# Layer 2 of the first two output tiles in seven block products, in a two-layer MLP with a residual

## The reference

```python
IN, HID, OUT, PART, E = (512, 2048, 512, 128, 8)
x = ...                         # (16, 512, 512) float32
itok_B_0_7 = ...                # 16 indices in 0..7
...
h = jax.nn.gelu(jnp.einsum('bni,ih->bnh', x, W1) + b1, approximate=False)
shared_x = jnp.einsum('bnh,ho->bno', h, W2) + b2      # W2: 2048 x 384
expert_x = jnp.einsum('bnh,bhp->bnp', h, We[indices]) + be[indices][:, None, :]   # 2048 x 128
return x + jnp.concatenate([shared_x, expert_x], axis=-1)
```

## Time and profile before

| | us |
|---|---|
| median of 3 runs (1288.54 to 1289.84) | 1289.72 |
| the profiled execution | 1288.96 |
| its span, first to last instruction | 1287.2 |
| PE busy | 1271.1 |
| DVE busy | 691.7 |
| ACT busy | 505.5 |
| moved by DMA | 62.23 MB, mean 48 GB/s |

### The profile page before, as it was taken

The page is one execution under the profiler, slowest core; times in us unless marked ns, Lnnn a source line. Parts: engine busy times, 40 slices in busy tenths (PEclk is TensorE's granted clock), DMA queues, the critical chain, the costliest instruction groups (busy, mean ns, idle before and its releaser), DMA issues.

```text
span 1287.2 us, 21032 instructions
## 1 busy us (share of the span) xinstructions
PE 1271.1 (99%) x8387; PEld 818.7 (64%) x8387; DVE 691.7 (54%) x860; ACT 505.5 (39%) x812; POOL 0.2 (0%) x4
## 2 busy tenths in 40 slices
PE   7999999999999999999999999999999999999998
PEld 3446666666666666666666666666666666666664
DVE  6965753745546455554645537455464555546442
ACT  3744444343343433343434443433434333434331
POOL 0000000000000000000000000000000000000000
PEclk8999999999999999999999999999999999999999
DMA  7121202011020110202001020110201102120000
GB/s 294 66 66 58 74 34 67 33 40 48 18 57 33 53 45 8 57 33 65 33 24 41 33 65 33 39 47 20 57 33 53 45 8 57 33 65 33 17 17 33
DMA packets 25081, 62.23 MB, mean 48 GB/s; under 512 B 5088, under 2 KB 5088, under 8 KB 21984
## 3 DMA queue, kind: packets, MB, share of 16 engines
q1 hardware_dynamic: 25056, 61.90, 15.1%
HBM read 45.11 MB, written 16.78 MB: 48 GB/s over the span
## 4 chain that ended last, share of the span: by engine, by line
PE 97%; DVE 2%; ACT 0%; issue 0%; ACTq 0%
PE out_ps L855 17%; PE out_ps L856 17%; PE out_ps L857 17%; PE banks L855 15%; PE banks L857 15%; PE banks L856 15%; DVE w_lo L543 1%; PE out_ps L990 1%; DVE w_max L529 0%; DVE x_lo L543 0%; DVE h_ring L543 0%; DVE x_max L529 0%; DVE e_lo L543 0%; ACT u L412 0%; ACT w_hi L369 0%
## 5 line engine op out<-in xcount | busy, mean ns | idle before, releaser
L855 PE MATMUL banks<-x_hi,w_hi 128*128 128x256 f16 (+1 forms) x1744 | 483.4, 277 | 7.6 <-DVE w_lo L543 5.0
L856 PE MATMUL banks<-x_lo,w_hi 128*128 128x256 f16 (+1 forms) x1744 | 483.2, 277 | 0.0
L857 PE MATMUL banks<-x_hi,w_lo 128*128 128x256 f16 (+1 forms) x1744 | 483.2, 277 | 0.0
L855 PE MATMUL out_ps<-h_ring,w_hi 128*128 128x512 f16 x768 | 291.0, 379 | 1.5 <-DVE w_lo L543 1.5
L857 PE MATMUL out_ps<-h_ring,w_lo 128*128 128x512 f16 x768 | 291.0, 379 | 0.0
L856 PE MATMUL out_ps<-h_ring,w_hi 128*128 128x512 f16 x768 | 291.0, 379 | 0.0
L404 ACT ACTIVATE kept<-banks 128x512 f32<-128x512 f32 x180 | 106.2, 590 | 366.2 <-PE banks L857 366.2
L855 PEld LDWEIGHTS banks<-x_hi,w_hi 128*128 128x128 f16 x1744 | 170.8, 98 | 80.1 <-DVE w_lo L543 5.2
L856 PEld LDWEIGHTS banks<-x_lo,w_hi 128*128 128x128 f16 x1744 | 170.9, 98 | 71.1 <-issue 1.1
L857 PEld LDWEIGHTS banks<-x_hi,w_lo 128*128 128x128 f16 x1744 | 170.9, 98 | 27.4 <-issue 1.4
L720 DVE TENSOR_TENSOR u<-banks,kept 128x512 f32<-128x512 f32 x60 | 41.5, 692 | 234.0 <-ACT kept L404 234.0
(11 more groups left out here) (90 smaller groups left out, 781.3 us busy)
## 6 DMA issues: line engine op xcount, KB each, us to landing
x_raw<-x_dram SPq DMA_DIRECT2D x64, 256.0 KB, 3.5
e_raw<-we_dram SPq DMA_DIRECT2D x16, 1024.0 KB, 4.7
out_dram<-x_raw SPq DMA_DIRECT2D x64, 256.0 KB, 2.0
stage<-w_dram SPq DMA_DIRECT2D x4, 1024.0 KB, 4.9
h_ring<-w_dram SPq DMA_DIRECT2D x2, 1024.0 KB, 8.6
stage<-w_dram SPq DMA_DIRECT2D x2, 768.0 KB, 14.4
x_raw<-w_dram SPq DMA_DIRECT2D x1, 1024.0 KB, 11.0
t_sum<-w_dram SPq DMA_DIRECT2D x1, 1024.0 KB, 12.5
```

What stands on the lines that cost most here:

```text
L855: nc.tensor.matmul(ps, hi, v_hi, start=start, stop=False, skip_group_check=True)
L856: nc.tensor.matmul(ps, hi, v_lo, start=False, stop=False, skip_group_check=True)
L857: return nc.tensor.matmul(ps, lo, v_hi, start=False, stop=stop, skip_group_check=True)
```

## The change

From batch 2 on (`PLAIN = 2`), layer 2 of output tiles 0 and 1 is computed by the same seven-product scheme: the 256 output columns by 512 tokens are a 2 by 2 of blocks, and the sum over the hidden features of a group likewise. It needs sums and differences of the blocks of h and of W2:

- `h_split`'s hi moves from VectorE to ScalarE for all batches. VectorE then makes four differences of blocks in place in `u` (`add_ht`, four adds of 128 x 512), ScalarE their hi, VectorE their lo (`ht_split`, 128 x 2048 each). `h_ring` now holds two groups of two parts.
- The sums of W2 are made once, in batch 2, from W2 loaded a second time (`reload_w2`, `add_w2_s`, `w2_s_split`).
- PSUM: `banks` shrinks to A and B (P5 and P3 take B, so P5 now waits for `c11` and P2 for `c12` of the step before), `out_ps` to two banks (o = 2 and 3); the seven products add up in four banks `q_ps`. `mix` (VectorE) puts them together: five passes of 128 x 256 for bank 2, two each for banks 0, 1 and 3; `q_keep` (ScalarE) copies the eighth block.
- A group's layer 2 is now 15 units: P1, P2, P6, P5, P7, P4 (six matmuls of 256 columns each), eight plain units of three matmuls with 512 columns for o = 2 and 3, then P3. `Q_UNITS` spreads them 2, 2, 3, 2, 2, 2, 2.
- The orders on VectorE and ScalarE change; `residual` moves from step 1 to step 0. The warm-up matmuls at the start become 60 and 30 with 256 columns instead of 32 and 14 with 512. The h scale has a smaller exponent.

```diff
+PLAIN = 2
-WARM, WARM_MORE = 32, 14
+WARM, WARM_MORE = 60, 30
...
-BANK_A, BANK_B, BANK_C = range(3)
-BANK = {P1: BANK_A, P2: BANK_B, P6: BANK_A, P5: BANK_C, P7: BANK_A, P4: BANK_A, P3: BANK_C}
+BANK_A, BANK_B = range(2)
+BANK = {P1: BANK_A, P2: BANK_B, P6: BANK_A, P5: BANK_B, P7: BANK_A, P4: BANK_A, P3: BANK_B}
...
+Q_PLACE = {P1: (0, 0), P2: (0, 1), P6: (1, 0), P5: (1, 1), P7: (2, 0), P4: (2, 1), P3: (3, 0)}
+Q_OPENS = (P1, P6, P7, P3)
 UNITS = (2, 2, 3, 2, 2, 3, 2)
+Q_UNITS = (2, 2, 3, 2, 2, 2, 2)
...
@@ scalar: h_split, ht_split, batch
+                nc.scalar.activation(h_ring[:, d % 2, 0, 0], u[:, d % 2].rearrange("p c n -> p (c n)"), ACT.Copy,
+                                     scale=scale[:, par, 1:2]).then_inc(h_hi_done, 1)
...
+                act.wait_ge(ht_added, 4 * (D * (b - PLAIN) + d) + 4)
+                nc.scalar.activation(h_ring[:, d % 2, 1, 0], u[:, d % 2].rearrange("p c n -> p (c n)"), ACT.Copy,
+                                     scale=scale[:, par, 1:2]).then_inc(ht_hi_done, 1)
...
                 keep(b, 0, 0)
+                h_split(b - 1, 1 - par, 3)
                 keep(b, 0, 1)
+                ht_split(b - 1, 1 - par, 3)
+                residual(b, par)
                 keep(b, 0, 2)
...
@@ vector: add_ht, mix (bank 2), batch (steps 1 to 3)
+                nc.vector.tensor_tensor(b11, b12, b11, ALU.subtract).then_inc(ht_added, 1)
+                dve.wait_ge(ht_added, base + 1)
+                nc.vector.tensor_tensor(b12, b22, b12, ALU.subtract).then_inc(ht_added, 1)
+                dve.wait_ge(ht_added, base + 2)
+                nc.vector.tensor_tensor(b22, b22, b11, ALU.subtract).then_inc(ht_added, 1)
+                dve.wait_ge(ht_added, base + 3)
+                nc.vector.tensor_tensor(b21, b21, b22, ALU.subtract).then_inc(ht_added, 1)
...
+                elif bank == 2:
+                    dve.wait_ge(q_taken, 4 * k + 2)
+                    take(c22, P7, c22).then_inc(q_mixed, 1)
+                    take(u_mix[:, :], P7, u_mix[:, :]).then_inc(q_mixed, 1)
+                    take(c21, P4, c21).then_inc(q_taken, 1)
+                    dve.wait_ge(q_mixed, 5 * k + 4)
+                    nc.vector.tensor_tensor(c22, c22, w_mix[:, :], ALU.add).then_inc(q_mixed, 1)
+                    dve.wait_ge(q_taken, 4 * k + 3)
+                    nc.vector.tensor_tensor(c21, c21, u_mix[:, :], ALU.add).then_inc(out_ready[1], 1)
...
+                c11(b, 1)
+                h_split(b, 0, par)
                 e_scales(b, par)
-                finish(b - 1, 1 - par, 0)
+                add_ht(b, 0)
+                mix(b - 1, 1 - par, 0)
                 e_split(b, 0)
+                e_split(b, 1)
+                ht_split(b, 0, par)
...
                 c22(b, 1)
...
+                c11(b, 2)
+                h_split(b, 1, par)
+                mix(b - 1, 1 - par, 2)
+                add_ht(b, 1)
+                finish(b - 1, 1 - par, 2)
                 finish(b - 1, 1 - par, 3)
-                c11(b, 2)
+                mix(b - 1, 1 - par, 3)
+                ht_split(b, 1, par)
...
                 c22(b, 2)
...
                 if loads is not None:
                     x_top(b + 1, 1 - par, loads)
-                h_split(b, par, 2)
                 c11(b, 3)
+                h_split(b, 2, par)
                 if loads is not None:
                     x_scales(b + 1, 1 - par)
+                add_ht(b, 2)
+                if loads is not None:
+                    add_t(b + 1, 1 - par)
                     x_split(b + 1, 1 - par, P1)
                     x_split(b + 1, 1 - par, P2)
-                    add_t(b + 1, 1 - par)
-                e_split(b, 3)
+                ht_split(b, 2, par)
                 c22(b, 3)
...
@@ tensor: layer1, plain_unit, product_unit
                 if i == P2 and begun:
-                    pe.wait_ge(c11_added, s)
-                if i == P5 and begun:
                     pe.wait_ge(c12_added, s)
+                if i == P5:
+                    pe.wait_ge(c11_added, s + 1)
...
+                first, last = d == 0 and c == 0, d == D - 1 and c == C - 1
...
+                if first and not (isinstance(b, int) and b == 0):
+                    pe.wait_ge(out_ready[o], b)
...
+                bank, n = Q_PLACE[i]
+                if d == 0 and n == 0:
+                    if not (isinstance(b, int) and b == PLAIN):
+                        pe.wait_ge(q_taken, 4 * (b - 1 - PLAIN) + bank + 1)
```

More of the change, by code:

```diff
@@ L180, in build, with place @@
         residual_done = sem("residual_done")
[L181 to L185, removed]
+        plain_summed = sem("plain_summed")
+        o_summed = sem("o_summed")
+        q_summed = sem("q_summed")
+        q_kept = sem("q_kept")
+        q_taken = sem("q_taken")
+        q_mixed = sem("q_mixed")
+        out_ready = [sem(f"out_ready{o}") for o in range(OT)]
+        def place(r, part):
+            return h_ring[:, r, part].rearrange("p a n -> p (a n)").bitcast(F32)
         def w1_raw(d):
@@ L289, in _ @@
             load_w1(3)
-            for d in range(D):
-                load_w2(d)
+            load_w2(0)
+            load_w2(1)
+            load_w2(3)
+            sp.wait_ge(w1_lo_done, 2)
+            load_w2(2)
             load_expert(0, 0)
@@ L740, in batch @@
+            def batch(b, par, loads=None, sums=False, w2_s=False):
                 c11(b, 0)
+                h_split(b - 1, 3, 1 - par)
+                add_ht(b - 1, 3)
                 e_top(b)
+                ht_split(b - 1, 3, 1 - par)
                 if sums:
                     add_s(1)
+                if w2_s:
+                    add_w2_s(0)
                 c22(b, 0)
-                c12(b, 0)
                 if sums:
                     s_split(1)
-                h_split(b, par, 0)
+                if w2_s:
+                    w2_s_split(0)
+                c12(b, 0)
@@ L841, in _ @@
             batch(1, 1, 1, sums=True)
+            batch(2, 0, 2, w2_s=True)
             with dve.Fori(0, B // 2 - 2) as pair:
-                batch(2 * pair + 2, 0, pair + 2)
                 batch(2 * pair + 3, 1, pair + 2)
-            batch(B - 2, 0, B // 2)
+                batch(2 * pair + 4, 0, pair + 3)
             batch(B - 1, 1)
-            h_split(B - 1, 1, 3)
-            for o in range(OT):
-                finish(B - 1, 1, o)
+            h_split(B - 1, 3, 1)
+            add_ht(B - 1, 3)
+            ht_split(B - 1, 3, 1)
+            for bank in range(3):
+                mix(B - 1, 1, bank)
+            finish(B - 1, 1, 2)
+            finish(B - 1, 1, 3)
+            mix(B - 1, 1, 3)
         @block.tensor
@@ L924, in layer2 @@
                 v = slice(c * N, (c + 1) * N)
[L925 to L934 removed]
+                ps = q_ps[:, o].rearrange("p j n -> p (j n)") if o < 2 else out_ps[:, o - 2]
@@ L998, in _ @@
             pe.wait_ge(w2_lo_done, D)
-            for d in range(D):
-                step(1, d)
-            with pe.Fori(2, B - 1) as b:
+            for b in (1, 2):
+                for d in range(D):
+                    step(b, d)
+            with pe.Fori(3, B - 1) as b:
                 for d in range(D):
@@ L1006, in _ @@
             for d in (D - 2, D - 1):
-                for unit in range(OT * C):
+                for unit in range(sum(Q_UNITS)):
                     layer2(B - 1, d, unit)
```

387 lines of the change are left out of this document (273 added, 114 removed).

## The result

| | before | after |
|---|---|---|
| median, us | 1289.2 | 1394.74 |
| ratio, with its 95% interval | | 1.082 (1.0807 to 1.0832) |
| profiled execution, us | 1288.96 | 1393.71 |
| its span, us | 1287.2 | 1391.9 |
| mean granted clock | 0.997 | 0.979 |

Each median is that of four runs; those of the change lie between 1393.71 and 1396.12 us.

The account below looks back on a forecast made before the run. PE's own rate was taken as the bound. From 1289.7 us, savings of 33.0 and 0.4 against waits of 84.0 and 11.0 in the loop, 6.85 in batch 2 and 5.3 at the end gave +73.7: 1363 us, range 1325 to 1395.

Parts of the forecast that it names:

- the course given 0.74: The main forecast: PE waits in the loop as walked through each step, 1363 us, own range 1345 to 1387, chance 0.74.
- the clock rival: Step 2's two gaps bring PE's clock to its low level each batch, costing 2.6 x 14 = 36 us: 1400, chance 0.11.
- three signs of being wrong: PE waiting under 2.4 us a batch, a 256-column pass far from 0.48, or granted clock leaving 1.0 in the loop.
- The saving on PE: Layer 2, batches 2 to 15: seven products replace eight units, 0.6 us a step over 56 groups, 33 us.
- The walk: PE's waits traced through each step: 4.46 us in step 2, 1.6 in step 0, 0.4 in step 1, 0.85 in step 3.
- step 2, P7 of layer 2 for `mix`: In step 2, PE waits for the `mix` passes that free this product's bank: 1.74 us a batch.
- step 2, o = 2 for `finish`: In step 2, PE waits for `finish` to free the bank of o = 2: 2.72 us more a batch.
- The three small terms of batch 2: Batch 2's W2 sums: `c22` 3.15 us late in step 1, bank A's GELU held 0.7, step 2 late by 3.0.
- The start-up order: The start-up's new order costs nothing: VectorE has the same work and the moved hi falls into a ScalarE wait.
- The x load: The next x, loaded behind later stores, costs nothing: some 22 against 22.9, with 2 us more of slack.
- only step 2's wait is real: Rival: the waits of steps 0, 1 and 3 vanish as errors of long sums; 1327 us, chance 0.10.
- PE stays fed: Rival: VectorE delivers in time, all loop waits are zero and the saving comes whole; 1262 us, chance 0.05.

Follow-up runs that it names:

- e7: e6 with the last group's plain units ahead of its products and the last four stores in the order their outputs come: 1258.0 us, ratio 0.9756.
- e1: The changed kernel with `mix` of banks 2 and 3 and both `finish` moved on VectorE from step 2 to the end of step 1: 1306.45 us, ratio 1.0131.
- e4: The changed kernel with `residual` ahead of the second hi split of h on ScalarE in step 0: 1362.26 us, ratio 1.0572.
- e5: The changed kernel with the last W1 reload ahead of batch 0's store of o = 2 on the sync queue: 1388.09 us, ratio 1.0773.
- e3: The changed kernel with only the two `finish` (o = 2 and 3) moved to the end of step 1 on VectorE: 1350.09 us, ratio 1.047.
- e6: The changed kernel with the moves of e1 and e4 and three more reorderings, the same work: 1263.24 us, ratio 0.9799.
- e2: The changed kernel with only `mix` of bank 2 moved to the end of step 1 on VectorE: 1358.83 us, ratio 1.0533.
- e8: The changed kernel with 32 unused 128-column matmuls added at the end of step 1 from batch 3 on: 1407.81 us, ratio 1.0914.

## Why the prediction was right, and where it fell short

**What held, and what was luck.** The waits that make up the sum were there, and the kernel is slower for the reason given. That 1394.74 us still lies in the range is luck: the range ended at 1395, one fall of the clock more would have left it, and two of the four runs lie above it. It lies outside 1345 to 1387, the range of the course given 0.74, and next to the 1400 of the clock rival, given 0.11. One of the three signs of being wrong came true: the granted clock left 1.0 inside the loop.

**The saving on PE** (33 us): right, and shown by e7. From 1289.06 to 1258.0 are 31.1, with the start-up's and the end's small costs in it. From `c11` to `c11` a batch lasted 78.17 us before and lasts 75.87 in e7, 2.3 less where 2.4 was expected; 14 x 2.3 = 32.

**The walk** (from start to start, us a batch):

| | walked | trace of after |
|---|---|---|
| step 2, P7 of layer 2 for `mix` | 1.74 | 1.60 + 0.16 |
| step 2, o = 2 for `finish` | 2.72 | 2.62 + 0.16 |
| step 0, P4 for the third copy | 1.6 | 1.49 + 0.16 |
| step 1, P3 for `c22` | 0.4 | 0.30 + 0.16 |
| step 3, P3 for `c22` | 0.85 | 0.73 + 0.16 |
| end, last group for h lo | 3.1 | 3.02 + 0.16 |

Each is right within 0.1 us. The 256-column passes cost 0.48 and 0.42, as interpolated from the 512 and 2048-column ones. The page "VectorE: DVE Perf Modes" of the Trainium skill (section "The TRN2 errata — SBUF-src ops pay a fixed extra latency per instruction") gives (N + 151)/0.96 ns for a float32 `tensor_tensor` add, measured there at 512 and 2048 columns. An estimate by it for 256 columns is 424 ns, and the trace agrees with 0.42. At the end, the four queued stores took from the last add at 1387.33 to 1391.9, 4.6 us against 2.6 before: the 2 us assumed. The three small terms of batch 2 were 3.15, 0.7 and 3.0 in the walk and 2.68, 0.70 and 3.10 in the trace. VectorE's share was put near 75% and came to 68%: a batch has 58.4 us of its work, not 61.

**The clock** was the step that failed. The sum has no term for it; I gave it 0.11 as a rival, and all that stood against it was one gap in the start-up of before, of 2.6 us, that had left the clock at 1.0. It fell in 12 of 14 batches. One such gap is no ground: the same one brought the clock down in four of the runs above. Its price per fall was oversized in turn: 2.6 us from "low for some 5 us", where it stays low for 3.4 us and loses 1.7. A batch with a fall lasts 85.08 us (565.83 to 650.91) and one without 83.45 (1076.30 to 1159.75), so 1.65 each, 20 us in all. What the rival had right: e1 shows that the low clock is paid in full beside the waits. The page "TensorE: Matmul & The Clock Gate" of the Trainium skill, in the section that the prediction weighed ("What's actually happening"), says that low is the default and activity releases it. That fits, but by itself does not tell between 12 falls and 2 behind the same gaps, as the change and e4 have.

**The start-up order** was costed at nothing: 4.4 us of wait and 1.7 of clock in batch 1, shown by e5 (6.65). The step missed is that a moved `finish` also moves its store, and with it everything behind that store on the sync queue.

**The x load** was costed at nothing with a slack of 3 us. In the change that was nearly right (8.9 us of VectorE waits, hidden but for 0.4 us in one batch); in e3 it was not.

Together: 12 x 1.65 + 6.1 (4.4 + 1.7) + 1.7 for the clock at the end = 27.6 of the 31.0 us missing (1393.71 - 1288.96 - 73.7). The rest is small errors of the walk: without a fall a batch is 83.45 - 78.17 = 5.3 longer than before, where 4.9 was walked, 5 us in 13 batches, of which the start-up and the small terms give some back.

**The rivals.** That only step 2's wait is real is out: e6 took the others away for what they were priced at. That PE stays fed is out for this order, and true for e7's.

## What to carry to other kernels

When work moves off the bound engine on to idle ones, their busy shares say little. Write down when the bound engine wants each result, and walk the in-order queue that makes it. Here some 28 us a batch of idle VectorE time, (1391.9 - 943.4) / 16, did not help, because a few short instructions that PE waited for stood behind work that was not wanted for half a step. Results that free a bank or a buffer belong as early in the queue as their inputs allow, and work for the next step behind the copies that the present step waits for. What an instruction releases on other queues, a store and the loads behind it, moves with it.

## What the runs showed of the hardware that I had not expected

- The granted clock fell to its lower level behind two gaps of PE of 1.8 and 2.8 us (start to start) with 1.3 us of matmuls between, and in 3 of 14 batches behind a single gap of 2.8. A single gap of 1.8 brought it down in none of 13 batches (e3). The gap at the end, 3.2 us start to start, did so in all eight kernels that have it. The clock stayed low for 3.4 us (6.8 in batch 1 of e2 and e4), at a loss of 1.65 to 1.7 us of PE's time.
- The same two gaps brought it down in 12 of 14 batches with a batch of 83.5 us without a fall, in 2 of 14 with one of 81.8 (e4), and in 8 of 14 with one of some 85.4 (e8). So the time of a kernel with gaps of this size moves by more than its waits explain: by 17 us here from the change to e4, and by some 5 us from run to run of one version (e4 and e8).
